# A graph and expert network on one core: the expert loop rolled for all experts, and scatters straight from the record columns

## What is computed

```python
h = gelu(x @ W1[e] + b1[e], approximate=False)
out = out + gate[:, e] * (h @ W2[e] + b2[e])
```

## Time and profile before

| | us |
|---|---|
| median of 3 runs | 4744.22 (4742.98 to 4748.11) |
| span of the profiled execution | 5102.1 |
| first expert stage, first load to next stage's first issue | 1687.8 to 2725.5 |
| second expert stage, first load to last tile added | 4712.7 to 5086.95 |

### The profile page before, as it was taken

One profiled execution on the slowest core, in us unless ns is written; L12 is line 12 of the kernel. 1 busy time (PEld: TensorE's weight loads), 2 busy tenths in 40 slices (PEclk: granted clock), 3 DMA queues, 4 the chain that ended last, 5 costly groups with the idle time before them and its releaser, 6 DMA issues. The chain is left out here.

```text
span 5102.1 us, 58668 instructions
## 1 busy us (share of the span) xinstructions
PE 2674.1 (52%) x11127; PEld 1856.8 (36%) x11128; DVE 1893.5 (37%) x4714; ACT 1149.0 (23%) x3778; POOL 2164.1 (42%) x2734
## 2 busy tenths in 40 slices
PE   3223945665542399999203777774100001635898
PEld 2123923333321277777102333333100000423676
DVE  5600265656557711111002222223444445465411
ACT  0010022222210111111001111111466666310111
POOL 0165045555530665565562666660466665000000
PEclk8555556666655699999656666665555555555999
DMA  2111422222220000000001333330000000000000
GB/s 71 40 41 60 181 55 76 79 78 76 72 59 0 25 10 17 9 20 1 1 1 41 90 88 88 90 90 17 5 5 5 5 5 4 0 0 11 19 9 25
DMA packets 118123, 199.51 MB, mean 39 GB/s; under 512 B 54417, under 2 KB 81158, under 8 KB 115910
## 3 DMA queue, kind: packets, MB, share of 16 engines
q0 software_dynamic: 75360, 124.95, 10.1%
q1 hardware_dynamic: 42726, 74.12, 4.2%
HBM read 186.58 MB, written 12.36 MB: 39 GB/s over the span
## 5 line engine op out<-in xcount | busy, mean ns | idle before, releaser
L493 POOL DMA_INDIRECT a0rows<-table,a0idx x462 | 469.6, 1016 | 517.6 <-ACT a0idx L478 403.8
L493 POOL DMA_INDIRECT a1rows<-table,a1idx x444 | 421.5, 949 | 325.3 <-ACT a1idx L478 175.5
L950 POOL DMA_INDIRECT erecords<-sc_slot x416 | 408.5, 982 | 328.3 <-POOL sc_slot L946 311.7
L523 PE MATMUL a1ps<-a1rows,a1w 128*128 128x256 f32 x888 | 428.1, 605 | 191.9 <-DMA a1rows<-table,a1idx 135.3
L523 PE MATMUL a0ps<-a0rows,a0w 128*128 128x257 f32 x924 | 416.3, 585 | 177.0 <-DMA a0rows<-table,a0idx 82.7
L1146 POOL DMA_INDIRECT gt_land<-table_gat,gt_idx x324 | 356.8, 1101 | 249.9 <-POOL gt_idx L1141 162.2
L1341 ACT ACTIVATE gt_parts<-gt_nb,gt_land 128x128 f32 x1296 | 414.8, 392 | 20.7 <-DVE gt_parts L1191 1.8
L1363 PE MATMUL gt_psT<-k_ident,gt_top 128*128 128x128 f32 x100 | 27.9, 434 | 702.2 <-DVEq L1196 702.2
L749 PE MATMUL f0dn<-f0w,f0hid 128*128 128x256 f32 x1600 | 353.3, 380 | 61.9 <-DVE k_x L797 61.9
L523 PEld LDWEIGHTS a1ps<-a1rows,a1w 128*128 128x128 f32 x888 | 212.0, 279 | 408.1 <-issue 283.5
L764 PE MATMUL f0up<-k_xnT,f0w 128*128 128x320 f32 x1280 | 352.9, 435 | 12.8 <-DMA f0b<-in_f_b 12.8
(11 more groups left out here) (366 smaller groups left out, 4185.1 us busy)
## 6 DMA issues: line engine op xcount, KB each, us to landing
es_ea<-in_eaT SPq DMA_DIRECT2D x16, 1664.0 KB
es_lane<-lane_row SPq DMA_DIRECT2D x16, 832.0 KB
f0w<-in_f_W SPq DMA_DIRECT2D x16, 512.0 KB
a0rows<-table,a0idx POOLq DMA_INDIRECT x462
a1rows<-table,a1idx POOLq DMA_INDIRECT x444
erecords<-sc_slot POOLq DMA_INDIRECT x416
table<-k_tbl SPq DMA_DIRECT2D x10, 650.0 KB, 3.5
gt_land<-table_gat,gt_idx POOLq DMA_INDIRECT x324
```

The source lines that it names most:

```text
L493: pool.indirect_dma_start(rows[:, i, 0:TW], None, table, bass.IndirectOffsetOnAxis(ap=idx[:, i:i + 1], axis=0)).then_inc(gathered[i], 16)
L523: nc.tensor.matmul(sum_of(t), w[:, i, :], rows[:, i, 0:width], start=False, stop=False).then_inc(agg_done, 1)
L950: pool.indirect_dma_start(self.rec_dram, bass.IndirectOffsetOnAxis(ap=slot[:, i, 0:1], axis=0), slot[:, i, 1:R + 1], None).then_inc(self.p ...
```

## The change

Three things change, all in the two expert stages and all the scatters of the first.

1. **One PE body for all experts and groups.** The loops over experts and over groups are both loops of the program; the body is one step, 8 matmuls of 384 columns and 8 of 256 for the ups (tiles 0 to 2, then 3 and 4), then 20 for the downs. A step's downs follow its own ups. Weights must then lie in one place: SP loads into `next1` and `next2`; DVE copies W1 over to `w1` when the last ups of the expert before are done, ACT copies W2 to `w2` when its last downs are done. There are five PSUM buffers for downs and two of one bank for ups.
2. **Bias per tile.** b1 comes in one load for all experts; ACT copies four columns of it for each expert. b2's adds come in groups of five, ahead of the five tiles of their step.
3. **Direct scatters.** The 80 + 416 scatters are written out without a loop, and each takes index and data straight from the record column. There is no copy to a slot. Scatter `sa` of the earlier stage stays as it was.

The diff's new lines follow; those that it takes away stand above, in the kernel before.

```diff
+    PER = 2 * KH
+    HALVES = ((0, 3), (3, U))
     W1, b1, W2, b2 = A[tag + "_W1"], A[tag + "_b1"], A[tag + "_W2"], A[tag + "_b2"]
+    arrived1, arrived2, small, live1, live2 = (sem(f"{tag}_{n}") for n in ("w1", "w2", "small", "live1", "live2"))
+    up_done, hid_ready, down_done, added = (sem(f"{tag}_{n}") for n in ("up", "hid", "down", "add"))
     with ExitStack() as ctx:
         sb = lambda n, s, d: ctx.enter_context(nc.sbuf_tensor(tag + n, s, d))
...
+        w1, next1 = sb("w1", [P, KD, H0], F32), sb("w1n", [P, KD, H0], F32)
+        w2, next2 = sb("w2", [P, KH, D], F32), sb("w2n", [P, KH, D], F32)
+        bias1, bias_now = sb("b1", [P, n_experts, KH], F32), sb("b1now", [P, KH], F32)
+        hid = [sb(f"hid{i}", [P, KH, (b - a) * P], F32) for i, (a, b) in enumerate(HALVES)]
         b2_rows = sb("b2", [P, n_experts, D], F32)
...
+        up = [ctx.enter_context(nc.psum_tensor(f"{tag}up{i}", [P, 512], F32)) for i in range(2)]
+        down = [ctx.enter_context(nc.psum_tensor(f"{tag}dn{i}", [P, 512], F32)) for i in range(U)]
         block = ctx.enter_context(nc.Block())
+
+        def add_tiles(v, e, g):
+            x_of = lambda j: S.x[:, bass.ds(g * (U * D) + j * D, D)]
+            gate_of = lambda j: gate[:, bass.ds(g * U + j, 1), bass.ds(e, 1)].rearrange("p a b -> p (a b)")
+            for j in range(U):
+                nc.vector.scalar_tensor_tensor(x_of(j), b2_rows[:, bass.ds(e, 1), :].rearrange("p a d -> p (a d)"), gate_of(j),
+                                               x_of(j), ALU.mult, ALU.add)
+            v.drain()
+            for j in range(U):
+                v.wait_ge(down_done, U + (e * OUT + g) * U + j + 1)
+                nc.vector.scalar_tensor_tensor(x_of(j), down[j][:, 0:D], gate_of(j), x_of(j), ALU.mult, ALU.add).then_inc(added, 1)
+            v.drain()
 
         @block.sync
         def _(sp):
...
+            def load(e):
+                sp.dma_start(next1[:], W1[bass.ds(e, 1), :, :].rearrange("a (k p) h -> p (a k) h", p=P)).then_inc(arrived1, 16)
+
+            def load2(e):
+                sp.dma_start(next2[:], W2[bass.ds(e, 1), :, :].rearrange("a (k p) d -> p (a k) d", p=P)).then_inc(arrived2, 16)
+
+            load(0)
+            load2(0)
+            with nc.allow_non_contiguous_dma(reason="biases, one element to a partition"):
+                sp.dma_start(bias1[:], b1.rearrange("e (k p) -> p e k", p=P)).then_inc(small, 16)
+            sp.dma_start(b2_rows[:], b2.unsqueeze(0).to_broadcast([P, n_experts, D])).then_inc(small, 16)
+            with sp.Fori(1, n_experts) as e:
+                sp.wait_ge(live1, e)
+                load(e)
+                sp.wait_ge(live2, e)
+                load2(e)
             for scatter in beside:
                 scatter.finish(sp)
 
@@ -738,67 +754,72 @@
 
         @block.tensor
         def _(pe):
...
+            pe.sem_inc(down_done, U)
+            with nc.Fori(0, n_experts, engines=[pe.engine], head_slot={pe.engine: 0}) as e:
+                with pe.Fori(0, OUT) as g:
+                    turn = e * OUT + g
+                    pe.wait_ge(live1, e + 1)
+                    for half, (a, b) in enumerate(HALVES):
+                        size = (b - a) * P
+                        for m in range(KH):
+                            q = half * KH + m
+                            pe.wait_ge(hid_ready, turn * PER + q + 1)
+                            for k in range(KD):
+                                ins = nc.tensor.matmul(up[q % 2][:, 0:size], w1[:, k, m * P:(m + 1) * P],
+                                                       S.xnT[:, k, bass.ds(g * (U * P) + a * P, size)],
+                                                       start=(k == 0), stop=(k == KD - 1))
+                            ins.then_inc(up_done, 1)
+                    pe.wait_ge(live2, e + 1)
+                    for half, (a, b) in enumerate(HALVES):
+                        pe.wait_ge(hid_ready, turn * PER + (half + 1) * KH + 2)
+                        for j in range(a, b):
+                            pe.wait_ge(added, turn * U + j + 1)
+                            for k in range(KH):
+                                ins = nc.tensor.matmul(down[j][:, 0:D], hid[half][:, k, (j - a) * P:(j - a + 1) * P],
+                                                       w2[:, k, :], start=(k == 0), stop=(k == KH - 1))
+                            ins.then_inc(down_done, 1)
 
         @block.scalar
         def _(act):
             nc.scalar.preload_act_table(ACT.Gelu)
...
+            act.sem_inc(hid_ready, 2)
+            act.wait_ge(small, 32)
+            with act.Fori(0, n_experts) as e:
+                act.wait_ge(down_done, U + e * NT)
+                act.wait_ge(arrived2, e * 16 + 16)
+                nc.scalar.copy(w2[:], next2[:]).then_inc(live2, 1)
+                nc.scalar.copy(bias_now[:].unsqueeze(1), bias1[:, bass.ds(e, 1), :])
+                act.drain()
+                with act.Fori(0, OUT) as g:
+                    turn = e * OUT + g
+                    for half, (a, b) in enumerate(HALVES):
+                        act.wait_ge(down_done, turn * U + b)
+                        for m in range(KH):
+                            q = half * KH + m
+                            act.wait_ge(up_done, turn * PER + q + 1)
+                            nc.scalar.activation(hid[half][:, m, :], up[q % 2][:, 0:(b - a) * P], ACT.Gelu,
+                                                 bias=bias_now[:, m:m + 1]).then_inc(hid_ready, 1)
 
         @block.vector
         def _(v):
...
+            def weights_over(e):
+                v.wait_ge(up_done, e * (OUT * PER))
+                v.wait_ge(arrived1, e * 16 + 16)
+                nc.vector.tensor_copy(w1[:], next1[:]).then_inc(live1, 1)
+
+            v.sem_inc(added, U)
+            v.wait_ge(arrived1, 16)
+            nc.vector.tensor_copy(w1[:], next1[:]).then_inc(live1, 1)
+            v.wait_ge(small, 32)
+            with v.Fori(0, n_experts - 1) as e:
+                with v.Fori(0, OUT - 1) as g:
+                    add_tiles(v, e, g)
+                weights_over(e + 1)
+                with v.Fori(OUT - 1, OUT) as g:
+                    add_tiles(v, e, g)
+            with v.Fori(n_experts - 1, n_experts) as e:
+                with v.Fori(0, OUT) as g:
...
+class DirectScatter:
+    def __init__(self, nc, S, tag, rec, rec_dram, first, last, rec_sb=None):
+        self.nc, self.rec, self.rec_dram, self.rec_sb = nc, rec, rec_dram, rec_sb
+        self.first, self.last = first, last
+        self.back = S.sem(tag + "_back")
+        self.put = [S.sem(f"{tag}_put{i}") for i in range(8)]
+    def run(self, pool):
+        R = self.rec.shape[2]
+        for c in range(self.first, self.last):
+            turn, lane = divmod(c - self.first, 8)
+            if turn:
+                pool.wait_ge(self.put[lane], 16 * turn)
+            pool.indirect_dma_start(self.rec_dram, bass.IndirectOffsetOnAxis(ap=self.rec[:, c + 1, 0:1], axis=0),
+                                    self.rec[:, c + 1, 1:R], None).then_inc(self.put[lane], 16)
+    def finish(self, sp):
+        for i in range(8):
+            sp.wait_ge(self.put[i], 16 * ((self.last - self.first) // 8))
         if self.rec_sb is not None:
             sp.dma_start(self.rec_sb[:], self.rec_dram.rearrange("(p c) r -> p c r", p=P)).then_inc(self.back, 16)
             sp.wait_ge(self.back, 16)
...
 
             emit_layernorm_project(nc, S, "l1", wg, NE0, True, gate_scores)
             emit_top2_mask(nc, S)
-            beside = (Scatter(nc, S, "sb", recg, rec_dram, EARLY, GC, S.rec_sb, stage),
-                      Scatter(nc, S, "sc", rece, erec_dram, 0, NC, S.erec_sb, stage))
+            beside = (DirectScatter(nc, S, "sb", recg, rec_dram, EARLY, GC, S.rec_sb),
+                      DirectScatter(nc, S, "sc", rece, erec_dram, 0, NC, S.erec_sb))
             emit_experts(nc, S, "f0", A, NE0, S.gate0, beside)
         end_stage()
 
```

More of the change, by code:

```diff
@@ L699, in emit_experts @@
     sem = S.sem
-    STEPS, HALF = 2 * OUT, U * P // 2
-    arrived = [sem(f"{tag}_w{i}") for i in range(2)]
-    up_done, hid_ready, down_done, added, b2_in = (sem(f"{tag}_{n}") for n in ("up", "hid", "down", "add", "b2"))
+    PER = 2 * KH
+    HALVES = ((0, 3), (3, U))
     W1, b1, W2, b2 = A[tag + "_W1"], A[tag + "_b1"], A[tag + "_W2"], A[tag + "_b2"]
+    arrived1, arrived2, small, live1, live2 = (sem(f"{tag}_{n}") for n in ("w1", "w2", "small", "live1", "live2"))
+    up_done, hid_ready, down_done, added = (sem(f"{tag}_{n}") for n in ("up", "hid", "down", "add"))
@@ L773, in _ @@
             nc.scalar.preload_act_table(ACT.Gelu)
-            act.sem_inc(hid_ready, 1)
-            with act.Fori(0, n_experts // 2) as o:
-                for s in range(STEPS):
-                    act.wait_ge(down_done, 1 + o * (STEPS * U) + max(s - 1, 0) * U)
-                    for m in range(KH):
-                        act.wait_ge(up_done, o * (STEPS * KH) + s * KH + m + 1)
```

(3 more changed lines are left out.)

86 lines of the change are left out of this document (4 added, 82 removed).

## The result

The change takes **4392.7 us** (median of 4 runs, 4381.3 to 4402.3) where the kernel before takes 4745.6 (4 runs, 4743.0 to 4748.1): the ratio is 0.9252, 95% interval 0.9235 to 0.9268, 353 us less. The profiled execution of the change has a span of 4400.5 us and an own time of 4402.3, so this profile has none of the excess of 358 us that the one of before has. Predicted were 4515 us, 4400 to 4630: right in sign, 122 us too slow, and 7 us outside the range.

What follows compares the result with a forecast made beforehand. POOL's scatters were taken to bound the first expert stage, PE the second. Terms of -318 and -11 gave -329, cut by 100 for profile excess to -229: 4515 us, range 4400 to 4630.

Steps and rivals of the forecast that it cites:

- What bounds the kernel, and the sum: Both expert stages: POOL bounds the first, PE the second; after the change PE bounds both; -318 and -11, sum -329 us.
- From the profile to the runs: Profiled span 5102.1 against runs of 4744.2: 100 of 358 us excess put in the first expert stage, cutting -329 to -229.
- the prediction's other number, 4415: Run time in us predicted if the 358 us excess lies wholly outside the first expert stage.
- The copy's wait goes: First expert stage, POOL: copy and 0.76 us wait vanish, leaving 0.98 + 0.30 = 1.28 us per scatter, 496 scatters in 635.
- the gap stays: Rival, 12%: the 0.76 us belongs to the scatter, pitch falls only to 1.74, POOL stays the bound; -125, 4619 us.
- 51 us lost to bias adds: First expert stage: 80 us of DVE bias adds cost POOL's scatters 51 us, putting POOL's end at 2375.
- The rival by which the runs block whole: Rival, 6%: runs of 2.0 us of bias adds hold POOL for their whole length; its part ends at 2418; 4527 us.
- The first gelu, 9 us: Start of first expert stage: first gelu waits for all of b1 in one load, +9 us on PE, bounds 0 and 14.
- 0.2 us per turn: PE's ups wait for the gelu two back: 0.2 us lost per turn, +8 us in the first stage, +4 in the second.
- Copies of weights at nothing: Expert stages: DVE's w1 copy hides behind 8.6 us of downs, ACT's w2 copy behind 2.6 us of ups; no cost.
- the excess is POOL's tail: Rival, 5%: all 358 us lie in POOL's tail, so POOL really ends before PE; only 45 and 11 won; 4688 us.
- slower: the short loop starves PE: Rival, 5%: PE's loop turns back 60 times instead of 6, each fetching code for 6.1 us, +366; 4881 us.

## Why the prediction was right or wrong

- **What bounds the kernel, and the sum.** Right on the first kind of chip. The sum of the parts was -329 and the measured difference is -353. The stages give -327 and -17 for the predicted -318 and -11.
- **The step that failed is "From the profile to the runs".** It put 100 of the 358 us of excess into the first expert stage, by its share of POOL's instructions, and said that no row says where. Next to none of it lay there (1035.6 against 1037.7 us in the two profiles); 302 us lay ahead of the first expert stage and 51 between the two. Rows with idle time ending in issue pointed there, though only the second profile shows how much of that idle time is excess. Without that step the prediction's other number, 4415, stands 22 us from the result.
- **The copy's wait goes.** Right: 0.30 in place of 0.76. A scatter has 0.96 + 0.30 = 1.26 for the 1.28 taken, and "the gap stays" is refuted.
- **51 us lost to bias adds.** Wrong in size. The first scatter starts at 1384.0 and the read-back is issued at 2017.1, 633 us for 496 x 1.266 = 628. Of the 496 scatters 17 take 1.05 us or more, 1.34 at most, and all of it comes to some 5 us; most of the 40 runs of five adds lengthen none. The price was taken from runs of 25 adds, which do hold a scatter for 7 us; it is not in proportion to the length of the run. The rival by which the runs block whole falls too. The Trainium skill (SBUF — State Buffer, on the two separate sides) has whichever of the two engines starts first keep the shared ports for its whole instruction, and the other blocked. An add here is 0.41 us: the scatter held for 7 us stood through some 17 of them, while its neighbour got through among them with 1.25, and the scatters beside five adds are at most 0.38 longer. By what rule the long runs hold one scatter stays open.
- **The first gelu, 9 us.** Mis-sized: PE waits 3.59 us before its third group, and 2.13 in the second stage for the 4 taken. The groups ahead of that wait lasted 5.48 us, at the lower clock (0.50 from 1388 to 1394 us), where the prediction gave PE 2.6. The load that came last was not b1, as the prediction has it: in the DMA view b1 lands 8.0 us after its issue and b2, issued behind it, 10.8 us after, and the waits of ACT and DVE are for both. With b2 ahead of most of b1, b2 lands 6.4 us after its issue in the second stage where it took 8.5.
- **0.2 us per turn.** Mis-sized: the loads of W1 go out 86.6 us apart, so a turn is 17.32 us, 0.07 more than 17.25, not 0.2. Over 40 turns that is 3 us, not 8. With the gelu this is the 11 us by which the stage (709) is shorter than predicted (720).
- **Copies of weights at nothing.** Right: PE's idle time at L768 in the whole stage is 15.6 us, 12.0 of them ahead of the first copy and 3.6 for the first gelu.
- **The rival "the excess is POOL's tail".** Refuted, by the same two profiles.
- **The rival "slower: the short loop starves PE".** It had the sign that the second kind of chip shows, and the wrong mechanism. PE is starved of instructions there, but with the old body of ten steps just the same (1313.8 and 1320.9 us). On the first kind 60 turns instead of 6 cost at most the 8 and 5 us between the two bodies. The Trainium skill (Runtime: NRT & Kernel Launch, on instruction fetch mechanics) has a stall at a taken branch that leaves the window; no run shows one here.

So the sum was right for the kind of chip that the runs shown came from, while the profile of before looks like the other kind: its span and its stages are those of the second, though no record names the chip that it came from. The sign itself depended on which chip the runs would use, so that it came out right is in part luck. That something of the kind was at work could be seen beforehand (a profile 358 us above its runs, PE idle for issue where indirect DMAs came 1.27 us apart), and had been called unexplained.

## What to carry to other kernels

A profile that is longer than the runs by more than a few per cent is a finding, not noise to be shared out: compare its stages and look for idle time that ends in issue before anything is taken off a sum. Removing a small wait from a queue of indirect DMAs can be a gain on one chip and a loss on another; leave some 0.2 us of other work between them (here a pitch of 1.48 us instead of 1.27) and time the kernel on more than one chip. Bias adds of 25 in a row on VectorE held a scatter for 7 us each; cut into fives they cost it 0.38 at most, and a drain after every five was enough.

## What the runs showed of the hardware that was not expected

- The same kernel takes 4747 and 4748 us on two chips, and 5099, 5105 and 5112 on three, each on one occasion. In the profiles of the kernel before, the difference is in the stages with dense indirect DMAs alone; where these are absent, or 1.94 us apart, the stages agree within 2 us.
- On the second kind, PE (and DVE and ACT beside it) gets instructions at a rate that falls when POOL issues an indirect DMA every 1.27 us (72 PE instructions in 200 us) or 1.38 us (148), and is nearly whole at 1.48 (789) and whole at 1.575 (834). POOL itself is slowed far less: at 1.27 its 496 scatters take 666 us in place of 631. By what path the scatters take this from the others stays open. The page counts the packets of two instruction queues, 7 and 19 of them in the change on either kind, so PE is not held by more loads of code, as far as these rows count them; nothing was run that would show the path.
- With a drain on POOL behind the MEMSET of 400 columns the next indirect DMA starts 1.47 us after the MEMSET's end; without the drain 0.17 us after it.
- The unspaced gathers and first scatters of the kernel before lose some 350 us on the second kind of chip; its windows and PE's idle time for issue look like those of the held expert stage, and spacing them was not tried.
